# Two products of 256 columns become one of 512 in the edge sums, and VectorE adds the two halves of the bank

## The chip, the cores and the metric

The kernel runs on one NeuronCore of a Trainium2 chip. The time is the device time of one execution in microseconds, the median of three runs. The engines are TensorE (PE in the profile, its weight loads PEld), VectorE (DVE), ScalarE (ACT), GpSimd (POOL) and SyncE (SP, which only issues transfers here).

## The reference

Two graph layers, each followed by a feed-forward block, on 6250 nodes of 256 features and 100,000 edges:

```python
x = x + L0_gnn(layernorm(x), src, dst, edge_weight)   # segment_sum(w * (x @ Wl)[src]) + x @ Wr + biases
x = x + L0_ffn(layernorm(x))                          # 8 experts, softmax gates, two hidden layers, BN + relu
x = x + L1_gnn(layernorm(x), src, dst, edge_weight)   # segment_sum(w * (x @ W)[src]) + bias
x = x + L1_ffn(layernorm(x))                          # 32 experts, argmax picks one, relu
```

In both graph layers `out[n]` is the sum over the edges that end in node n of the edge's weight times the row of the edge's source node (`jax.ops.segment_sum`). All of it is float32.

## The kernel before

The edges are sorted so that the edges of 128 nodes stand together, padded to 784 tiles of 128 edges. A slot s takes U = 4 tiles, so there are EGROUPS = 196 slots. The code writes the order of every engine by hand, slot by slot: a Python loop over s emits for PE, VectorE and ScalarE what belongs to the slot, and semaphores tie the engines together. Nothing is scheduled afterwards.

An edge sum is a matrix product: for 128 edges, a one-hot matrix (edge by node) is the weight operand and the 128 gathered rows are the moving operand; the product adds 256 columns for 128 nodes into a PSUM bank. For precision each float32 operand is split into an upper part (rounded to fp32r) and a lower part (the rest), and the parts are multiplied apart.

**Second stage, names f_...** GpSimd gathers four times 128 rows a slot (L1408, an indirect DMA each, ring of four slots in `got`). ScalarE multiplies them by the edge weights (L1467) and writes the upper part `mhi` (L1476); VectorE writes the lower part `mlo` (L1683) and the one-hot `hot` (L1677). PE multiplies the same one-hot by `mhi` and then by `mlo` into `bank[6 + t % 2]`, columns 0 to 255 (L1584, L1585). Edges of one slot can belong to two node tiles, so some slots have 4 such pairs and some 8: 1168 in all. When tile t is complete, in slot 4t+5, VectorE adds the bank to the node's row (L1807) and runs the layer norm's statistics (L1809 to L1813). The first FFN runs beside the edges, one expert in two slots: PE L1397 to L1399 (layers of up to 512 columns and outputs of 256), ScalarE relu and upper part (L1492, L1497), VectorE lower part (L1689) and the gated output add (L1706). VectorE's lower messages free the ring slot for GpSimd. After the last edges the FFN goes on alone until about 1790 us.

**Last stage, names n_...** The gathered rows are already two-part: a table row is 512 wide, upper part then lower part. VectorE writes weighted one-hots, upper `hot_h` and lower `hot_l` (L2360, eight instructions of 128 columns a slot). For every edge tile PE runs three products of 256 columns: `hot_h` by the upper half, `hot_h` by the lower half, `hot_l` by the upper half (L2231 to L2233), so 784 of each. The sums run over windows of two slots and 128 nodes that overlap by half, in `bank[6 + m % 2]`. When window m closes, ScalarE copies one half of 64 partitions to `agg` (L2171, `s_half`) and VectorE adds the other half, whose copy came from the window before (L2378, `s_sum`). PE opens a bank again two windows later, behind `s_half` and `s_sum`. Beside it the second FFN runs from slot 13 on: PE hidden products (L2249 to L2253), ScalarE relu (L2184), VectorE lower part n_hrl (L2394), PE outputs (L2273 to L2277). GpSimd's gathers (L2120, ring of four slots) wait for PE's count of slots, `s_prod`.

Of the kernel before, what the change touches and what calls it, by code (L numbers as in the profile page):

```python
# [9 lines left out]
F32R = mybir.dt.float32r  # L10
# [3 lines left out]
ALU = mybir.AluOpType  # L14
# [18 lines left out]
U = 4  # L33
# [57 lines left out]
def build(nc, x, src, dst, wgt, wl, wr, bl, br, gw, gbr, w1, b1, g1, be1, m1, v1,  # L91
          w2, b2, g2, be2, m2, v2, wo, bo, lw, lb, rw, rb, mw1, mb1r, mw2, mb2, out):
    ctx = ExitStack()
    with ctx:
# [1115 lines left out]
        with ExitStack() as c3, nc.Block() as block:  # L1210
# [8 lines left out]
            s_accin = sem("f_accin")  # L1219
            s_sum = sem("f_sum")  # L1220
# [53 lines left out]
            mhi = sb3("mhi", [P, 2, U, D], F32R)  # L1274
            mlo = sb3("mlo", [P, 2, U, D], F32R)
# [86 lines left out]
            def tile_bank(t):  # L1362
                return bank[6 + t % 2][:, 0:D]
# [207 lines left out]
            def _(pe):  # L1571
                def edges(s):
# [6 lines left out]
                    for u in range(U):  # L1579
                        for t, at in node_tiles(s):  # L1580
# [3 lines left out]
                            nc.tensor.matmul(tile_bank(t), lhs, mhi[:, s % 2, u, :], start=begins, stop=False)  # L1584
                            last = nc.tensor.matmul(tile_bank(t), lhs, mlo[:, s % 2, u, :], start=False, stop=ends)  # L1585
# [82 lines left out]
            def _(dve):  # L1668
# [109 lines left out]
                for s in range(SLOTS):  # L1778
# [22 lines left out]
                    for g in range(NG):  # L1801
                        for k in range(width(g)):
                            t = tile(g, k)
                            if edges_end(t) == s:
                                dve.wait_ge(s_prod, s)
                                dve.wait_ge(s_accin, g * 16 + 16)
                                nc.vector.tensor_tensor(row(g, k), tile_bank(t), row(g, k), ALU.add).then_inc(s_sum, 1)  # L1807
# [93 lines left out]
        with ExitStack() as c4, nc.Block() as block:  # L1901
# [16 lines left out]
            s_half = sem("n1_half")  # L1918
            s_lw = sem("n1_lw")
# [149 lines left out]
            def window_bank(m):  # L2069
                return bank[6 + m % 2][:, 0:D]  # L2070
# [89 lines left out]
            def _(act):  # L2160
# [3 lines left out]
                for s in range(SLOTS):  # L2164
                    if s % 2 == 1 and s < EGROUPS:
# [5 lines left out]
                        nc.scalar.activation(agg[a:b, t % 2, :], window_bank(m)[a:b, :], ACT.Copy).then_inc(s_half, 1)  # L2171
# [46 lines left out]
            def _(pe):  # L2218
                def edges(s):
                    m = window_of(s)  # L2220
                    opens, closes = s == 0 or s % 2 == 1, s % 2 == 0 or s == EGROUPS - 1
                    if opens and m >= 2:
                        pe.wait_ge(s_half, m - 1)
# [4 lines left out]
                    for u in range(U):  # L2228
                        w_h, w_l = hot_h[:, s % HOTS, u, :], hot_l[:, s % HOTS, u, :]
                        m_h, m_l = (got[:, s % RING, u, a:a + D] for a in (0, D))  # L2230
                        nc.tensor.matmul(window_bank(m), w_h, m_h, start=(opens and u == 0), stop=False)  # L2231
                        nc.tensor.matmul(window_bank(m), w_h, m_l, start=False, stop=False)  # L2232
                        last = nc.tensor.matmul(window_bank(m), w_l, m_h, start=False, stop=(closes and u == U - 1))  # L2233
# [105 lines left out]
            def _(dve):  # L2339
# [32 lines left out]
                for s in range(SLOTS):  # L2372
                    m = (s - 1) // 2
                    if s % 2 == 1 and 1 <= m < WINDOWS:
                        t, (a, b) = halves(m)[1]
                        dve.wait_ge(s_prod, min(s, EGROUPS))
                        dve.wait_ge(s_half, m)
                        nc.vector.tensor_tensor(agg[a:b, t % 2, :], window_bank(m)[a:b, :], agg[a:b, t % 2, :],  # L2378
                                                ALU.add).then_inc(s_sum, 1)
# [144 lines left out]
```

## Time and profile before

| | |
|---|---|
| median of 3 runs | 3136.0 us (3130.68 to 3143.77) |
| the profiled execution, its own time | 3133.19 us |
| span of its instructions | 3131.3 us |
| PE busy | 2684.4 us, 86% |
| PEld (weight loads) | 2474.8 us, 79% |
| DVE busy | 2161.1 us, 69% |
| ACT busy | 1557.7 us, 50% |
| POOL busy | 1971.0 us, 63% |
| mean granted TensorE clock | 0.929 |

Busy time is the union of an engine's instructions; the reported ends of matmuls are modelled and overlap the next one, so the distance between starts tells what a product costs. "Idle before" names what the engine waited for; "issue" is a wait for which the profile shows nothing, "remote" one for a releaser that it could not name.

### The profile page before, as it was taken

The page shows a single profiled execution, that of the slowest core. Times are in us where ns is not written, and L with a number is a line of the kernel's source. Part 1 is how long each engine was busy: PE and PEld are TensorE (multiplying, and loading weights), DVE is VectorE, ACT ScalarE, POOL GpSimd, SP SyncE. Part 2 cuts the span into 40 slices and gives each one's busy share as a digit, 9 for nine tenths or more (in the row PEclk, how much of TensorE's full clock was granted, in tenths as well). Part 3 has the DMA queues.
Part 4 walks back from the last instruction along what each step waited for, and adds up shares of the span by engine and source line. Part 5 has one row for each costly group of instructions (what it writes and reads, how often), then busy time and mean ns, then how long its engine had stood idle before and what let it go on. Part 6 is the DMA issues. An engine that isn't in the chain of part 4 may idle for free. (4 is left out here: it accounts for less than half of the span.)

```text
span 3131.3 us, 54480 instructions
## 1 busy us (share of the span) xinstructions
PE 2684.4 (86%) x19092; PEld 2474.8 (79%) x19092; DVE 2161.1 (69%) x5110; ACT 1557.7 (50%) x3295; POOL 1971.0 (63%) x1696
## 2 busy tenths in 40 slices
PE   5899826899999999999999737888888989888889
PEld 5788725798888888888888626788888888888889
DVE  8888654588787878778876565665666666666663
ACT  3477555788888888888886410111111111111112
POOL 0455467678888888888880076666666666666660
PEclk9999957899999999999999967899998999899999
DMA  2143453233333332333231176767776776767760
GB/s 70 6 94 77 101 156 105 82 93 110 93 101 109 108 111 83 110 108 112 86 110 35 36 226 172 183 172 179 179 178 172 179 175 176 181 176 179 178 171 13
DMA packets 241962, 390.31 MB, mean 125 GB/s; under 512 B 43642, under 2 KB 115218, under 8 KB 241426
## 3 DMA queue, kind: packets, MB, share of 16 engines
q0 software_dynamic: 163072, 310.24, 38.6%
q1 hardware_dynamic: 78324, 74.90, 7.7%
q8 instruction: 156, 2.56, 0.3%
q10 hardware_dynamic: 288, 1.61, 0.1%
q14 instruction: 122, 1.00, 0.1%
HBM read 343.43 MB, written 43.19 MB: 123 GB/s over the span
## 5 line engine op out<-in xcount | busy, mean ns | idle before, releaser
L1408 POOL DMA_INDIRECT f_got<-h_tab,list_cols x784 | 991.5, 1265 | 251.4 <-issue 221.3
L2120 POOL DMA_INDIRECT n_got<-h_tab,edge_cols x784 | 807.9, 1031 | 427.9 <-issue 220.5
L2184 ACT ACTIVATE n_hrh<-bank 128x512 fp32r<-128x512 f32 x196 | 117.0, 597 | 644.3 <-DMA list<-runs,off_i 355.0
L1689 DVE TENSOR_TENSOR f_hlo<-edge_cols,f_hhi 128x1024 fp32r<-128x1024 f32 (+1 forms) x208 | 241.9, 1163 | 259.6 <-ACT f_hhi L1497 189.1
L2394 DVE SCALAR_TENSOR_TENSOR n_hrl<-bank,n_hrh 128x512 fp32r<-128x512 f32 x196 | 135.1, 689 | 379.6 <-ACT n_hrh L2184 305.8
L1467 ACT ACTIVATE f_got<-f_got,list_cols 128x256 f32<-128x256 f32 x784 | 333.4, 496 | 116.3 <-DMA f_got<-h_tab,list_cols 110.9
L1584 PE MATMUL bank<-f_mhi,f_hot 128*128 128x256 f32 x1168 | 307.3, 296 | 56.9 <-DVE f_mlo L1683 50.6
L1492 ACT ACTIVATE edge_cols<-bank,f_shf,f_scl 128x512 f32<-128x512 f32 (+1 forms) x416 | 292.1, 743 | 94.4 <-PE bank L1399 39.7
L2231 PE MATMUL bank<-n_got,n_hot_h 128*128 128x256 f32 x784 | 244.0, 311 | 79.9 <-DMA n_got<-h_tab,edge_cols 36.7
L1585 PE MATMUL bank<-f_mlo,f_hot 128*128 128x256 f32 x1168 | 305.4, 295 | 3.5 <-issue 3.5
L400 POOL DMA_INDIRECT list<-runs,off_i x98 | 159.9, 1631 | 217.5 <-DVE off_i L759 100.4
L1584 PEld LDWEIGHTS bank<-f_mhi,f_hot 128*128 128x128 f32 x1168 | 235.3, 201 | 63.5 <-issue 59.5
L2249 PE MATMUL bank<-n_xnh,n_w1h 128*128 128x256 f32 (+1 forms) x800 | 238.4, 298 | 22.0 <-ACT n_ohT L2206 11.8
L1397 PE MATMUL bank<-f_whi,f_hhi 128*128 128x256 f32 x784 | 230.2, 294 | 27.5 <-DVE f_hlo L1689 19.2
L1683 DVE TENSOR_TENSOR f_mlo<-f_got,f_mhi 128x1024 fp32r<-128x1024 f32 x196 | 238.7, 1218 | 17.7 <-ACT f_mhi L1476 17.3
L2275 PE MATMUL bank<-n_w2l,n_hrh 128*128 128x256 f32 x784 | 229.3, 292 | 24.4 <-issue 24.3
L2251 PE MATMUL bank<-n_xnh,n_w1l 128*128 128x256 f32 (+1 forms) x800 | 236.2, 295 | 11.1 <-issue 10.8
L2273 PE MATMUL bank<-n_w2h,n_hrh 128*128 128x256 f32 x784 | 230.0, 293 | 17.8 <-issue 17.3
L2250 PE MATMUL bank<-n_xnl,n_w1h 128*128 128x256 f32 (+1 forms) x800 | 236.5, 296 | 6.6 <-issue 6.4
L1585 PEld LDWEIGHTS bank<-f_mlo,f_hot 128*128 128x128 f32 x1168 | 235.1, 201 | 8.7 <-issue 5.0
L2360 DVE TENSOR_SCALAR n_hot_h<-list_cols,rel_f,edge_cols 128x128 fp32r<-128x128 f32 x784 | 220.4, 357 | 28.3 <-remote 17.8
L2277 PE MATMUL bank<-n_w2h,n_hrl 128*128 128x256 f32 x784 | 227.6, 290 | 13.7 <-issue 12.9
(329 smaller groups left out, 7882.4 us busy)
## 6 DMA issues: line engine op xcount, KB each, us to landing
f_got<-h_tab,list_cols POOLq DMA_INDIRECT x784
n_got<-h_tab,edge_cols POOLq DMA_INDIRECT x784
n_rows<-acc_tab SPq DMA_DIRECT2D x24, 256.0 KB
out_rows<-n_rows SPq DMA_DIRECT2D x24, 256.0 KB
h_tab<-acc SPq DMA_DIRECT2D x37, 128.0 KB
edge_cols<-in_w SPq DMA_DIRECT2D x16, 256.0 KB
acc<-in_x SPq DMA_DIRECT2D x4, 896.0 KB
h_tab<-hbuf SPq DMA_DIRECT2D x7, 512.0 KB
```

Source lines behind the costliest of these rows:

```text
L1408: nc.gpsimd.indirect_dma_start(got[:, s % RING0, u, :], None, h_tab[0], bass.IndirectOffsetOnAxis(gidx0[:, s * U + u:s * U + u + 1], 0), b ...
L1467: last = nc.scalar.activation(got[:, s % RING0, u, :], got[:, s % RING0, u, :], ACT.Copy, scale=w0_f[:, c:c + 1])
L1492: nc.scalar.activation(rl[:, m, 0:w], bank[(i + m) % 3][:, 0:w], ACT.Relu, bias=shf[:, l, e, m:m + 1], scale=scl[:, l, e, m:m + 1]).then_i ...
L1584: nc.tensor.matmul(tile_bank(t), lhs, mhi[:, s % 2, u, :], start=begins, stop=False)
L1585: last = nc.tensor.matmul(tile_bank(t), lhs, mlo[:, s % 2, u, :], start=False, stop=ends)
L1683: nc.vector.tensor_tensor(mlo[:, s % 2, :, :], got[:, s % RING0, :, :], mhi[:, s % 2, :, :].bitcast(F32), ALU.subtract).then_inc(s_mlo, 1)
L1689: nc.vector.tensor_tensor(hlo[l][:, :, 0:w], rl[:, :, 0:w], hhi[l][:, :, 0:w].bitcast(F32), ALU.subtract).then_inc(s_lo[l], 1)
L2120: nc.gpsimd.indirect_dma_start(got[:, s % RING, u, :], None, h_tab[1], bass.IndirectOffsetOnAxis(gidx[:, s * U + u:s * U + u + 1], 0), bou ...
L2231: nc.tensor.matmul(window_bank(m), w_h, m_h, start=(opens and u == 0), stop=False)
L2249: nc.tensor.matmul(to, hi_w, hi_x, start=(f == 0), stop=False)
L2250: nc.tensor.matmul(to, hi_w, lo_x, start=False, stop=False)
L2251: nc.tensor.matmul(to, lo_w, hi_x, start=False, stop=False)
```

## The change

In the second stage upper and lower messages lie side by side in one tile `msg`, and one product of 512 columns writes a whole bank: columns 0 to 255 get the upper part's sum, 256 to 511 the lower part's. VectorE adds first the one half of the bank to the row, then the other, with a wait between them (`s_upsum`). In the last stage `hot_h` meets the whole gathered row in one product of 512 columns, and `hot_l` the upper half as before into columns 0 to 255. ScalarE copies its half of the partitions from columns 0 to 255. VectorE then adds, for each window: columns 0 to 255 of the half it has always added; columns 256 to 511 of the half that ScalarE copied (`s_low`, behind `s_half` of the same window); columns 256 to 511 of its own half (`s_sum`). PE opens the bank again behind `s_low` and `s_sum`.

```diff
-            mhi = sb3("mhi", [P, 2, U, D], F32R)
-            mlo = sb3("mlo", [P, 2, U, D], F32R)
+            msg = sb3("msg", [P, 2, U, 2 * D], F32R)
+            mhi, mlo = (msg[:, :, :, i * D:(i + 1) * D] for i in range(2))
...
-                            nc.tensor.matmul(tile_bank(t), lhs, mhi[:, s % 2, u, :], start=begins, stop=False)
-                            last = nc.tensor.matmul(tile_bank(t), lhs, mlo[:, s % 2, u, :], start=False, stop=ends)
+                            last = nc.tensor.matmul(tile_bank(t)[:, :], lhs, msg[:, s % 2, u, :], start=begins, stop=ends)
...
-                                nc.vector.tensor_tensor(row(g, k), tile_bank(t), row(g, k), ALU.add).then_inc(s_sum, 1)
+                                nc.vector.tensor_tensor(row(g, k), tile_bank(t)[:, 0:D], row(g, k), ALU.add).then_inc(s_upsum, 1)
+                                dve.wait_ge(s_upsum, t + 1)
+                                nc.vector.tensor_tensor(row(g, k), tile_bank(t)[:, D:2 * D], row(g, k), ALU.add).then_inc(s_sum, 1)
...
-                        nc.scalar.activation(agg[a:b, t % 2, :], window_bank(m)[a:b, :], ACT.Copy).then_inc(s_half, 1)
+                        nc.scalar.activation(agg[a:b, t % 2, :], window_bank(m)[a:b, 0:D], ACT.Copy).then_inc(s_half, 1)
...
-                        pe.wait_ge(s_half, m - 1)
+                        pe.wait_ge(s_low, m - 1)
...
-                        m_h, m_l = (got[:, s % RING, u, a:a + D] for a in (0, D))
-                        nc.tensor.matmul(window_bank(m), w_h, m_h, start=(opens and u == 0), stop=False)
-                        nc.tensor.matmul(window_bank(m), w_h, m_l, start=False, stop=False)
-                        last = nc.tensor.matmul(window_bank(m), w_l, m_h, start=False, stop=(closes and u == U - 1))
+                        ends = closes and u == U - 1
+                        nc.tensor.matmul(window_bank(m)[:, :], w_h, got[:, s % RING, u, :], start=(opens and u == 0),
+                                         stop=ends, skip_group_check=True)
+                        last = nc.tensor.matmul(window_bank(m)[:, 0:D], w_l, got[:, s % RING, u, 0:D], start=False,
+                                                stop=ends, skip_group_check=True)
...
-                    if s % 2 == 1 and 1 <= m < WINDOWS:
-                        t, (a, b) = halves(m)[1]
+                    if s % 2 == 1 and m < WINDOWS:
+                        copied, added = halves(m)
                         dve.wait_ge(s_prod, min(s, EGROUPS))
-                        dve.wait_ge(s_half, m)
-                        nc.vector.tensor_tensor(agg[a:b, t % 2, :], window_bank(m)[a:b, :], agg[a:b, t % 2, :],
-                                                ALU.add).then_inc(s_sum, 1)
+                        if added:
+                            t, (a, b) = added
+                            rest = agg[a:b, t % 2, :]
+                            dve.wait_ge(s_low, m)
+                            nc.vector.tensor_tensor(rest, window_bank(m)[a:b, 0:D], rest, ALU.add).then_inc(s_upsum, 1)
+                        if copied:
+                            t, (a, b) = copied
+                            dve.wait_ge(s_half, m + 1)
+                            nc.vector.tensor_tensor(agg[a:b, t % 2, :], window_bank(m)[a:b, D:2 * D], agg[a:b, t % 2, :],
+                                                    ALU.add).then_inc(s_low, 1)
+                        if added:
+                            t, (a, b) = added
+                            dve.wait_ge(s_upsum, m)
+                            nc.vector.tensor_tensor(rest, window_bank(m)[a:b, D:2 * D], rest, ALU.add).then_inc(s_sum, 1)
```

PE, last stage, the edges of one slot in the midst of the run (n_hot_h and n_hot_l are the one-hots, n_got the gathered rows). Before, the first two of its four edge tiles:

```order
L2231 MATMUL bank<-n_got,n_hot_h 128x256
L2232 MATMUL bank<-n_got,n_hot_h 128x256
L2233 MATMUL bank<-n_got,n_hot_l 128x256
L2231 MATMUL bank<-n_got,n_hot_h 128x256
L2232 MATMUL bank<-n_got,n_hot_h 128x256
L2233 MATMUL bank<-n_got,n_hot_l 128x256
```

Now the last three of the four, and the first output product of the FFN behind them:

```order
L2235 MATMUL bank<-n_got,n_hot_h 128x512
L2237 MATMUL bank<-n_got,n_hot_l 128x256
L2235 MATMUL bank<-n_got,n_hot_h 128x512
L2237 MATMUL bank<-n_got,n_hot_l 128x256
L2235 MATMUL bank<-n_got,n_hot_h 128x512
L2237 MATMUL bank<-n_got,n_hot_l 128x256
L2278 MATMUL bank<-n_w2h,n_hrh 128x256
```

A slot's twelve edge products have become eight; nothing around them moved.

VectorE, last stage, the start of an odd slot, in which a window closes (n_agg is the sum of a tile, n_xnl belongs to the slot before). Before:

```order
L2431 TENSOR_TENSOR n_xnl<-list_cols,n_xnh 128x2x128
L2378 TENSOR_TENSOR n_agg<-bank,n_agg 64x256
L2360 TENSOR_SCALAR n_hot_h<-list_cols,rel_f,edge_cols 128x128 x4
L2360 TENSOR_SCALAR n_hot_l<-list_cols,rel_f,edge_cols 128x128 x4
L2394 SCALAR_TENSOR_TENSOR n_hrl<-bank,n_hrh 128x512
```

Now:

```order
L2447 TENSOR_TENSOR n_xnl<-list_cols,n_xnh 128x2x128
L2386 TENSOR_TENSOR n_agg<-bank,n_agg 64x256
L2390 TENSOR_TENSOR n_agg<-bank,n_agg 64x256
L2395 TENSOR_TENSOR n_agg<-bank,n_agg 64x256
L2365 TENSOR_SCALAR n_hot_h<-list_cols,rel_f,edge_cols 128x128 x4
L2365 TENSOR_SCALAR n_hot_l<-list_cols,rel_f,edge_cols 128x128 x4
L2410 SCALAR_TENSOR_TENSOR n_hrl<-bank,n_hrh 128x512
```

Two more adds stand ahead of the one-hots and of n_hrl.

VectorE, second stage, a slot in which a tile is complete (f_msg holds both parts of the messages, f_xlo belongs to the FFN's next group). Before:

```order
L1677 TENSOR_TENSOR f_hot<-xn,rel_f 128x4x128
L1683 TENSOR_TENSOR f_mlo<-f_got,f_mhi 128x1024
L1799 TENSOR_TENSOR f_xlo<-edge_cols,f_xhi 128x1024
L1807 TENSOR_TENSOR acc<-bank,acc 128x256
L1809 BN_STATS f_stats<-acc 128x6
```

Now, in the same slot:

```order
L1677 TENSOR_TENSOR f_hot<-xn,rel_f 128x4x128
L1683 TENSOR_TENSOR f_msg<-f_got,f_msg 128x4x256
L1799 TENSOR_TENSOR f_xlo<-edge_cols,f_xhi 128x1024
L1807 TENSOR_TENSOR acc<-bank,acc 128x256
L1809 TENSOR_TENSOR acc<-bank,acc 128x256
L1811 BN_STATS f_stats<-acc 128x6
```

The second add stands between the first and the statistics; the lower messages (L1683) now go out in four pieces of 256.

## Rows read from the trace of the kernel before

**Rows 1.** The page, busy time of each engine.
```profile
PE 2684.4 (86%) x19092; PEld 2474.8 (79%) x19092; DVE 2161.1 (69%) x5110; ACT 1557.7 (50%) x3295; POOL 1971.0 (63%) x1696
```

**Rows 2.** Stretches: length, busy PE, PEld, DVE, ACT, POOL, clock, DMA share, GB/s.
```profile
1100.00:1600.00 500.00, 474.42 (x2977) 422.75 (x2977) 405.31 (x686) 437.25 (x701) 403.41 (x317) 0.99 0.35 105
2000.00:2500.00 500.00, 446.43 (x3300) 424.17 (x3299) 313.72 (x1110) 82.03 (x216) 321.26 (x316) 0.94 0.70 177
2500.00:3000.00 500.00, 441.82 (x3273) 422.25 (x3272) 311.57 (x1105) 82.55 (x217) 322.08 (x317) 0.94 0.71 178
3050.00:3131.00 81.00, 77.87 (x646) 76.78 (x645) 29.29 (x83) 16.29 (x37) 1.09 (x2) 1.00 0.07 20
```

**Rows 3.** Line L1408, 1100 to 1600 us: ns, idle before it, who waited.
```profile
L1408 POOL DMA_INDIRECT f_got<-h_tab,list_cols x317: 1011/1017/2821, 1099.6 to 1598.7; - x159
...
  issue: 89.9, 295
  DVE f_mlo L1683: 6.7, 22
...
  ACT f_got L1467: 29.6, 27
```

**Rows 4.** Timeline, 461 and 1151 us: start, length, engine, line.
```profile
461.70 0.42 DVE L1807 TENSOR_TENSOR acc<-bank,acc 128x256 f32<-128x256 f32 x1
461.84 1.01 POOL L1408 DMA_INDIRECT f_got<-h_tab,list_cols  x1 [0.30 <-DVE f_mlo L1683]
...
1151.53 1.22 DVE L1683 TENSOR_TENSOR f_mlo<-f_got,f_mhi 128x1024 fp32r<-128x1024 f32 x1
...
1152.20 1.43 POOL L1408 DMA_INDIRECT f_got<-h_tab,list_cols  x1 [0.30 <-issue]
...
1152.66 0.42 DVE L1807 TENSOR_TENSOR part<-bank,part 128x256 f32<-128x256 f32 x1
...
1153.12 0.43 DVE L1809 BATCH_NORM_STATS2 f_stats<-part 128x6 f32<-128x256 f32 x1
```

**Rows 5.** Waits of POOL and DVE, 2000 to 2500 us: us, times, longest.
```profile
DVE n_hrl L2394 <- ACT n_hrh L2184: 112.3, 36, 6.6
...
POOL n_got L2120 <- remote: 57.4, 27, 2.5
...
POOL n_got L2120 <- PE bank L2233: 32.8, 21, 2.8
```

**Rows 6.** Waits of PE, 2000 to 2500 us.
```profile
PE bank L2275 <- issue: 10.4, 16, 1.0
...
PE bank L2249 <- ACT n_ohT L2206: 6.7, 3, 3.2
```

**Rows 7.** Timeline, 2070 to 2075 us.
```profile
2070.41 0.38 ACT L2171 ACTIVATE n_agg<-bank 64x256 f32<-64x256 f32 x1 [1.46 <-remote]
2070.42 0.42 DVE L2378 TENSOR_TENSOR n_agg<-bank,n_agg 64x256 f32<-64x256 f32 x1 [0.96 <-remote]
...
2073.95 0.28 PE L2232 MATMUL bank<-n_got,n_hot_h 128*128 128x256 f32 x1 [0.33 <-issue]
...
2074.65 0.28 PE L2233 MATMUL bank<-n_got,n_hot_l 128*128 128x256 f32 x1 [0.41 <-issue]
```

**Rows 8.** Groups of instructions, whole span: count, busy us, mean ns, idle before.
```profile
L1585 PE MATMUL bank<-f_mlo,f_hot 128*128 128x256 f32 x1168 | 305.4, 295 | 3.5 <-issue 3.5
...
L2232 PE MATMUL bank<-n_got,n_hot_h 128*128 128x256 f32 x784 | 230.0, 293 | 7.0 <-issue 6.9
...
L2378 DVE TENSOR_TENSOR n_agg<-bank,n_agg 64x256 f32<-64x256 f32 x98 | 41.2, 420 | 39.4 <-remote 31.9 <-PE bank L2233 5.7
```

**Rows 9.** Timeline of PE, first and last of each run of even steps.
```profile
1199.77 0.39 PE L1398 MATMUL bank<-f_hlo,f_whi 128*128 128x512 f32 x1
...
1202.06 0.40 PE L1399 MATMUL bank<-f_hhi,f_wlo 128*128 128x512 f32 x1
...
1210.53 0.28 PE L1584 MATMUL bank<-f_mhi,f_hot 128*128 128x256 f32 x1
...
1211.48 0.28 PE L1397 MATMUL bank<-f_whi,f_hhi 128*128 128x256 f32 x1
```

More of the change, by code:

```diff
@@ L1219, in build @@
             s_accin = sem("f_accin")
+            s_upsum = sem("f_upsum")
             s_sum = sem("f_sum")
@@ L1362, in tile_bank @@
             def tile_bank(t):
-                return bank[6 + t % 2][:, 0:D]
+                return bank[6 + t % 2]
             def out_tile(k):
@@ L1918, in build @@
             s_half = sem("n1_half")
+            s_upsum = sem("n1_upsum")
+            s_low = sem("n1_low")
             s_lw = sem("n1_lw")
@@ L2069, in window_bank @@
             def window_bank(m):
-                return bank[6 + m % 2][:, 0:D]
+                return bank[6 + m % 2]
             def halves(m):
```

## The prediction

> **What bounds the kernel now.** I read the page first: TensorE (PE) is busy 86% of the span, VectorE (DVE) 69%, ScalarE (ACT) 50%, GpSimd (POOL) 63% [rows 1]. The average hides two different regimes, so next come the stretches. The change touches the "f" stage (edge sums of the first layer with the first FFN beside them, edges from about 410 to 1660 us) and the "n" stage (second layer, about 1812 to 3131 us).
>
> In the f stage, 1100 to 1600 us, PE is busy 474 of 500 us at clock 0.99, DVE 405, ACT 437, POOL 403 [rows 2]. POOL looks idle for a fifth of the time, but it is not: its waits are 89.9 us "issue" (295 times 0.30 us, the step between two gathers) and only 6.7 us for DVE [rows 3]. 403.4 + 89.9 = 493.3 of 500 us, so the issue of gathers sets the pace: 317 gathers, four to a slot, 6.31 us a slot. Behind it ACT waited for gathered rows 27 times, 29.6 us [rows 3]. PE's idle time is 25.6 us; it waits for ACT and DVE results of the FFN, which come late behind the gathers. Why a gather costs POOL 1.27 us there: its median is 1.017 us and its longest 2.82 [rows 3]. Where VectorE runs f_mlo (both operands in SBUF) while a gather starts, the gather ends 0.9 us after f_mlo does (1153.63 against 1152.75) and takes 1.43 us; where VectorE runs the add that reads a bank, it takes 1.01 us [rows 4]. So VectorE's operations on two SBUF operands stretch the gathers, and those with a bank operand don't.
>
> In the n stage, 2000 to 2500 us, 316 gathers make 79 slots of 6.33 us. PE is busy 446 us, its clock 0.94; DVE 314, ACT 82, POOL 321 [rows 2]. POOL waits there for PE: 57.4 (its "remote" is PE's count as well, the only thing it can wait for) + 32.8 us [rows 5], so PE leads. But 53.6 us of PE's idle time is mostly "issue" (the longest line 10.4 us), waits for which the profile shows no releaser; a real one is 6.7 us for ACT [rows 6]. They come in clusters while gathers run without a pause: two successive products start at 2073.95 and 2074.65, 0.70 us apart in place of 0.12, with nothing awaited [rows 7]. After the gathers end the stage has none of this: from 3050 us PE is busy 77.9 of 81 us at clock 1.00 [rows 2].
>
> **The change part by part.** PE. Each pair of 256-column products on the same weights becomes one of 512: 1168 pairs in f, 784 in n (196 slots of 4), and as many weight loads go [rows 8]. The reported 0.28 and 0.39 us of a product overlap its neighbours, so the price is the distance between starts. 256 columns: eight steps from 1210.53 to 1211.48, 0.119 us. 512 columns, same weight shape: ten steps from 1199.77 to 1202.06, 0.229 us [rows 9]. A pair costs 0.238 and the one product 0.229: 0.009 saved. The columns streamed are the same; only what a second start costs is saved. With the rounding of the starts (0.01 us over 8 and 10 steps) it lies between 0.007 and 0.011; I take 0.010.
> In f that is 1168 x 0.010 = 11.7 us of PE time. Until 1653 us it lies beside POOL, which is full. It counts 0, with a bound of 11.7 if PE turned out to set the pace. The FFN steps after the last edges have no such pair.
> In n it is 784 x 0.010 = 7.8 us. The second FFN does not begin before slot 13; until then PE has 12 short products a slot (1.4 us) against four gathers (5.2 us), so 13 x 4 pairs are hidden: 7.3 us on the path.
>
> The unexplained waits of n. A slot has 3300/79 = 41.8 products; the change takes 4 of them, 9.6%. Idle 53.6 and 58.2 us in the two stretches of 500 us [rows 2], less 6.7 us for ACT in the first and about as much in the second, is 98 us in 1000; the clock of 0.94 (12% of the time at half rate) adds 30 us in 500. Over the 1050 us from 2000 to 3050 that makes about 166 us. If these waits belong to PE's instruction count, 9.6% of it goes: 16 us. If they belong to the stream of gathers, which stays as it is, nothing goes. The trace does not decide. That the waits are gone where the gathers are [rows 2], and that the bytes moved are alike in both stretches (177 and 178 GB/s), speaks for the gathers. I take a third, 5 us, and keep 0 and 16 as ends.
>
> VectorE, f stage. One more add of the form bank + SBUF row, 128x256, for each of 49 tiles: 0.42 us, and 0.46 from its start to that of the next, dependent one (1152.66 to 1153.12 [rows 4]): 49 x 0.46 = 22 us. It stands behind f_mlo of the slot and ahead of bn_stats, where only the tile's own chain waits. Its operand is a bank, so by rows 4 it leaves the gathers alone. DVE has 95 of 500 us idle. Cost 0; if the cover were gone, up to 22 us. f_mhi and f_mlo are now written in pieces of 256 elements that lie 512 apart, the number of elements being the same; I count nothing for it. A tenth on f_mlo's 1.22 us would stretch 196 gathers by 0.12 us, 24 us: that is its upper end.
>
> VectorE, n stage. Before, one add of 64 partitions for a window, now three: 98 + 98 + 98, so 196 more at 0.42 (0.46 with the step), 90 us [rows 8]. It takes DVE from 314 to about 350 of 500 us. The order within an odd slot: add, add (behind ACT's copy of the same window), add, then the one-hots two slots ahead, then n_hrl. Queued behind the new wait are the one-hots and n_hrl. Two adds make n_hrl 0.9 us later; by the code PE asks for the n_hrl of slot s in slot s + 1, behind that slot's edges. DVE's largest idle time is before just this n_hrl, 112.3 us for ACT [rows 5], and it swallows the adds. ACT's copy (0.38 us) starts with DVE's first add, 2070.41 and 2070.42 [rows 7], so the new wait on it is empty. PE used to wait for the copy and the add, and now for one add more, two slots ahead of need: no cost. For the first windows, where slots are short, I count 1 us.
>
> Sum: 0 - 7.3 - 5 + 0 + 1 = -11.3 us. The profiled run took 3133.2 us (span 3131.3), which gives 3121.9. The median before is 3136.0, 2.8 us above the profiled run, so I forecast 3125 us.
>
> **The rivals.** (A) PE gains count in full: the waits without releaser shrink with the instruction count (16 us), and in f PE's 11.7 us is worth something because POOL, ACT and PE are within 5% of each other. For: PE is busy 95% in f. Against: POOL's 493.3 of 500. It gives -7.8 - 16 to -7.8 - 16 - 11.7, so 3100 to 3112 us.
> (B) Slower: the 0.455 us added in the 49 sum slots of f pushes the next two-SBUF operations (f_hot, f_mlo) onto the start of a gather that they now miss. The price is that of rows 4: 0.42 us for a gather that started 0.67 us into f_mlo, and up to 1.09 for one that starts with it. If each sum slot had one more blocked start, 49 x 0.42 to 1.09 = 21 to 53 us, less 12: 3145 to 3177 us. It decides from about two blocked starts in three sum slots on. Against: gathers are already stretched by 0.25 us on average, four to a slot, and a shift makes as many starts free as it blocks.
>
> (C) The n stage is paced by the gathers and not by PE: its 177 and 178 GB/s are what it gets. Then a faster PE only waits more, and the change gives 0 to -3 us: 3133 to 3136. For: the even rate. Against: POOL stands waiting for PE 90 of 500 us.
> The Trainium skill, "Runtime: NRT & Kernel Launch", section on instruction fetch mechanics, says that blocks of 256 instructions are fetched ahead and that crossing one is mostly hidden; by that the waits would not come from PE's instruction stream and the 5 us would be 0 (3130). No row here names their cause.
>
> **How the numbers follow.** My forecast 0.40, (A) 0.27, (B) 0.13, (C) 0.20. The measurement tells 0.5% (15.7 us) from no change, so faster begins below 3120.3 us and slower above 3151.7. Faster: most of (A), 0.25, and a quarter of the forecast's own spread (3112 to 3131), 0.10. Slower: two thirds of (B), and a little for a VectorE chain that is tighter than I see, 0.12. The rest, 0.53, is no change. The range: the forecast, (C), (A) down to 3102 and the lower part of (B), 3102 to 3148.
>
> **What would show it.** Right: starts of the 512-column products 0.227 to 0.230 us apart and 0.35 us for 512 plus 256 in n; gathers of f still at a mean near 1.27 us and POOL's issue plus busy near 493 of 500; PE's idle share in f higher by about 1 point; the f stage as long as before within 5 us; DVE up by some 36 us in 2000 to 2500 with no PE wait for n_agg; slots of n near 6.27 us. Wrong: PE waits "for DVE n_agg"; f_msg lines that hold the gathers longer (mean above 1.30); an n slot below 6.2 us, which would be (A); PE's waits for gathered rows in n, which would be (C); or steps of 0.238 us and more for the 512 columns.

## The result, and the profile after

| | before | after |
|---|---|---|
| median, on the same chip | 3143.4 us (7 runs, 3130.7 to 3155.2) | 3123.7 us (7 runs, 3115.7 to 3132.2) |
| ratio to before | 1 | 0.9946 (0.9923 to 0.9970) |
| the profiled execution | 3133.2 us | 3132.2 us |

The change makes the kernel 0.54% faster, 17 us by the ratio and 20 us by the medians. The forecast was 3125 us, 11 us less than before. The two profiled executions differ by 1 us only: that of after was the slowest of its seven runs. Their gathers, first start to last, take 1241.4 us before and 1238.1 after in f (the second stage), 1237.1 and 1236.5 in n (the last stage). So the two profiles tell what an operation costs and who waits for whom, and the 17 us have to be found with more runs.

The page of the kernel after, busy time of each engine (to [rows 1]):

```profile
PE 2679.6 (86%) x17140; PEld 2368.7 (76%) x17140; DVE 2264.5 (72%) x5355; ACT 1561.0 (50%) x3295; POOL 1966.8 (63%) x1696
```

PE has 1952 products fewer, 1168 + 784, and 4.8 us less busy time; DVE has 103 us more. The stretches of [rows 2], after:

```profile
1100.00:1600.00 500.00, 468.32 (x2481) 393.17 (x2480) 407.04 (x695) 432.85 (x693) 401.10 (x312) 0.98 0.34 104
2000.00:2500.00 500.00, 442.64 (x2961) 413.40 (x2960) 345.23 (x1173) 82.56 (x214) 317.88 (x315) 0.91 0.70 176
2500.00:3000.00 500.00, 447.90 (x2996) 413.27 (x2995) 350.16 (x1200) 84.04 (x220) 324.00 (x318) 0.92 0.70 178
```

In f, PE is idle 6 us more in 500 (474.4 became 468.3 busy). POOL issues 312 gathers in this stretch where it issued 317, but over the whole stage it is 3 us quicker, so no change of its pace can be read from that. In n, DVE has 31.5 us more in 500 and the same number of gathers goes through; PE's clock is 0.91 where it was 0.94. The f gathers of after in 1100 to 1600 us (to [rows 3]: least, median and longest ns, then the waits before them, then who waited for them):

```profile
L1409 POOL DMA_INDIRECT f_got<-h_tab,list_cols x312: 1007/1016/3232, 1099.4 to 1598.9; - x156
...
  issue: 89.7, 289
  DVE f_msg L1683: 9.5, 23
...
  ACT f_got L1468: 30.2, 29
```

401.1 + 89.7 = 490.8 of 500 us (493.3 before): POOL is still full, and its wait grew by 3 us. What a product of 512 columns costs, on PE's timeline of after in n (start, reported length, line):

```profile
2084.24 0.40 PE L2235 MATMUL bank<-n_got,n_hot_h 128*128 128x512 f32 x1
2084.47 0.28 PE L2237 MATMUL bank<-n_got,n_hot_l 128*128 128x256 f32 x1
2084.59 0.39 PE L2235 MATMUL bank<-n_got,n_hot_h 128*128 128x512 f32 x1
2084.82 0.27 PE L2237 MATMUL bank<-n_got,n_hot_l 128*128 128x256 f32 x1
2084.93 0.40 PE L2235 MATMUL bank<-n_got,n_hot_h 128*128 128x512 f32 x1
```

From 2084.24 to 2084.93 are two tiles, 0.345 us each, of which about 0.232 us for the 512 columns. Over all tiles of the stage the median step from L2235 to L2237 is 0.235 us, in f from one L1585 to the next 0.233; the median step of 256 columns before is 0.120. A pair saves 0.005 to 0.007 us, some 0.006, and not the 0.010 that I took: 5 us in n.

One wait is new, at the start of each group of the second FFN. Waits of PE after, 2000 to 2500 us (to [rows 6]):

```profile
PE bank L2254 <- ACT n_ohT L2210: 30.0, 8, 4.5
PE bank L2280 <- issue: 9.2, 12, 1.0
PE bank L2282 <- issue: 6.4, 11, 1.0
PE bank L2278 <- issue: 4.5, 6, 0.9
```

n_ohT is the one-hot of the chosen experts, ScalarE's last copy before a group's hidden products. PE waited 6.7 us for it in [rows 6] and 30.0 us here, 47.1 us over the stage against 11.8. (The expectations below speak of 98 us against 26: these add the waits of PE's weight loads, 51.2 and 14.6 us, which are largely the same time.) PE's waits without releaser fell at the same time, from 45.8 to 26.7 us in 2000 to 2500. Which of the two is the change's doing is a question for the runs.

POOL and VectorE after (to [rows 5]):

```profile
POOL n_got L2124 <- remote: 52.9, 24, 2.5
POOL n_got L2124 <- PE bank L2237: 46.3, 35, 2.3
```
```profile
DVE n_hrl L2410 <- ACT n_hrh L2188: 119.4, 50, 5.4
```

VectorE still stands 119 us for ScalarE before n_hrl, with 31.5 us more work. What became shorter are its other waits: those for a releaser without a name before n_agg (17.6 to 3.0 us) and before n_rows (13.1 us to none), and those without releaser before n_hrl (22.1 to 11.9). So the added adds seem to lie in idle time, though not in the wait for ScalarE.

### The profile page after: what moved, and what is told of

Its sections match the earlier page's. It is cut to its first block and busy times, and to the rows that moved or that the text cites. A ratio compares the mean times of both kernels' runs of the same rounds, so it can differ in the third digit from the quotient of the medians.

```text
span 3130.2 us, 50822 instructions
## 1 busy us (share of the span) xinstructions
PE 2679.6 (86%) x17140; PEld 2368.7 (76%) x17140; DVE 2264.5 (72%) x5355; ACT 1561.0 (50%) x3295; POOL 1966.8 (63%) x1696
## 5 line engine op out<-in xcount | busy, mean ns | idle before, releaser
L2235 PE MATMUL bank<-n_got,n_hot_h 128*128 128x512 f32 x784 | 326.8, 445 | 79.7 <-DMA n_got<-h_tab,edge_cols 35.5
L1585 PE MATMUL bank<-f_msg,f_hot 128*128 128x512 f32 x1168 | 325.3, 416 | 56.4 <-DVE f_msg L1683 48.1
L1585 PEld LDWEIGHTS bank<-f_msg,f_hot 128*128 128x128 f32 x1168 | 226.3, 201 | 107.8 <-issue 62.1
L2254 PE MATMUL bank<-n_xnh,n_w1h 128*128 128x256 f32 (+1 forms) x800 | 241.4, 302 | 58.2 <-ACT n_ohT L2210 47.1
L1683 DVE TENSOR_TENSOR f_msg<-f_got,f_msg 128x1024 fp32r<-128x1024 f32 x196 | 238.5, 1217 | 19.3 <-ACT f_msg L1477 17.8
L2235 PEld LDWEIGHTS bank<-n_got,n_hot_h 128*128 128x128 f32 x784 | 163.4, 208 | 115.6 <-issue 52.2
L2237 PE MATMUL bank<-n_got,n_hot_l 128*128 128x256 f32 x784 | 232.7, 297 | 2.2 <-issue 2.2
L2365 DVE TENSOR_SCALAR n_hot_l<-list_cols,rel_f,edge_cols 128x128 fp32r<-128x128 f32 x784 | 226.5, 369 | 0.0
```

What stands on the lines that cost most here:

```text
L1585: last = nc.tensor.matmul(tile_bank(t)[:, :], lhs, msg[:, s % 2, u, :], start=begins, stop=ends)
L2235: nc.tensor.matmul(window_bank(m)[:, :], w_h, got[:, s % RING, u, :], start=(opens and u == 0), stop=ends, skip_group_check=True)
L2237: last = nc.tensor.matmul(window_bank(m)[:, 0:D], w_l, got[:, s % RING, u, 0:D], start=False, stop=ends, skip_group_check=True)
L2254: nc.tensor.matmul(to, hi_w, hi_x, start=(f == 0), stop=False)
```

## The experiments

The first eight kernels ran on one chip (A) and the last four on another (B). Both are slower than the first: before takes 3189 to 3191 us on A and 3178 us on B. Only runs of one chip, or ratios to before on the same chip, are compared. The theories: **T**, mine: f is paced by POOL and gives nothing, all comes from n, the adds are hidden. **Rivals**: both stages give something (A of the prediction); n is paced by the gathers (C); the adds delay ScalarE and so cause the wait for n_ohT.

### Each stage alone

`e1_f_only` has the change in f and the code of before in n. `e2_n_only` is the other way round. Their diffs are the two parts of the diff above.

> Only the f stage is changed, the n stage is that of before. My theory (the issue of gathers sets the pace of f, 493 of 500 us, so PE's shorter pairs are hidden): 0 against before, at most 3 us either way; f gathers end within 4 us of before's (1242.5 us from first to last), gather mean near 1.26 us. Rival (A), PE's gain counts in f: -8 to -12 us, and the gathers end that much earlier. Rival (B), the added add stretches gathers: +20 us or more and a gather mean above 1.30.

> Only the n stage is changed. My theory: all of the difference of the changed kernel is here, so -11 to -20 us against before, as the whole change. Rival: the gain is split between the stages, then about half, -8 to -10 us. If the new waits of PE for ACT's n_ohT (98 us in the profile of the changed kernel against 26 us for the same step before) were a cost of their own, this kernel would be no faster than before.

Measured, with the whole change on the same chip: f alone 0.9963 (0.9933 to 0.9994, 12 runs), n alone 0.9943 (0.9918 to 0.9969, 12 runs), both 0.9922 (0.9893 to 0.9951, 8 runs):

> The changed kernel again, on the same chip as the experiments. From the two halves alone (0.9963 with f changed, 0.9943 with n changed) the sum is 0.9906; the first comparison gave 0.9946. If the stages add up, 0.989 to 0.993 here. My theory of step f = 0 gives 0.9943 (the n part alone).

So f gives some 12 us (between 2 and 21), n some 18 us (10 to 26), and the sum of the two, 0.9906, fits the 0.9922 of both. T is probably wrong on f, but not surely: the 2 us are within its "at most 3", and the interval of both holds its 0.9943 as well. The first and last gather of each stage (min/median/max ns, first and last start), f only, then n only, then both:

```profile
L1409 POOL DMA_INDIRECT f_got<-h_tab,list_cols x784: 1007/1015/3297, 408.0 to 1668.4; - x196
L2122 POOL DMA_INDIRECT n_got<-h_tab,edge_cols x784: 998/1004/3016, 1832.2 to 3094.6; - x196
```
```profile
L1408 POOL DMA_INDIRECT f_got<-h_tab,list_cols x784: 1006/1014/2859, 412.2 to 1685.8; - x196
L2122 POOL DMA_INDIRECT n_got<-h_tab,edge_cols x784: 997/1003/3532, 1852.4 to 3093.0; - x196
```
```profile
L1409 POOL DMA_INDIRECT f_got<-h_tab,list_cols x784: 1006/1014/2825, 410.4 to 1680.8; - x196
L2124 POOL DMA_INDIRECT n_got<-h_tab,edge_cols x784: 997/1003/3532, 1851.0 to 3094.2; - x196
```

n's gathers take 1262.4 us with the old products, 1240.6 and 1243.2 with the new ones: 20 us. (The two profiles of the first chip show 1 us of this.) f's take 1260.4 and 1270.4 with the new code, 1273.6 with the old: here two profiles of the same code differ by 10 us. The eight profiles of chip A have new code in f five times (mean 1265.8 us, 1258.5 to 1271.7) and old three times (1275.5, 1272.2 to 1280.7).

Where f loses time on this chip: POOL's waits from 500 to 1600 us, n only (f as before), then f only:

```profile
POOL f_got L1408 <- issue: 197.7, 622, 2.0
POOL f_got L1408 <- DVE f_mlo L1683: 69.1, 52, 8.7
```
```profile
POOL f_got L1409 <- issue: 197.7, 627, 2.0
POOL f_got L1409 <- DVE f_msg L1683: 51.4, 53, 8.2
```

The kernels before and after on the first chip have 26.8 and 22.3 us in that row. In this window POOL stands 2 us or longer, up to 9, in 14, 16 and 18 places in three profiles with f as before, and in 9, 10 and 13 places in three with f changed (1 and 2 on the first chip). The profile of both changes on chip A has 69.4 us in the row, as much as n only, so the row alone does not prove the gain. What such a place looks like: at 618 us in the profile of n only, gathers go on while PE starts its products 0.7 and then 1.4 us apart with nothing awaited, and ScalarE and VectorE stand as well:

```profile
618.29 0.39 PE L1398 MATMUL bank<-f_hlo,f_whi 128*128 128x512 f32 x1
...
619.01 0.48 PE L1399 MATMUL bank<-f_hhi,f_wlo 128*128 128x512 f32 x1 [0.33 <-issue]
...
620.43 0.48 PE L1397 MATMUL bank<-f_hhi,f_whi 128*128 128x512 f32 x1 [0.94 <-issue]
...
621.87 0.59 PE L1398 MATMUL bank<-f_hlo,f_whi 128*128 128x512 f32 x1 [0.96 <-issue]
...
630.53 1.06 ACT L1476 ACTIVATE f_mhi<-f_got 128x1024 fp32r<-128x1024 f32 x1 [10.70 <-remote]
```

This is what [rows 7] show in n. I read it so: after such a stop PE is late, POOL's ring is full, and then a lighter PE stream counts. That is argued from these places and not shown apart. My sum looked at a stretch with 6.7 us of such waits [rows 3] and priced f at 0 from it.

### The n stage without the added adds

```diff
-                            nc.vector.tensor_tensor(rest, window_bank(m)[a:b, 0:D], rest, ALU.add).then_inc(s_upsum, 1)
-                            nc.vector.tensor_tensor(agg[a:b, t % 2, :], window_bank(m)[a:b, D:2 * D], agg[a:b, t % 2, :],
-                                                    ALU.add).then_inc(s_low, 1)
-                            nc.vector.tensor_tensor(rest, window_bank(m)[a:b, D:2 * D], rest, ALU.add).then_inc(s_sum, 1)
+                            dve.sem_inc(s_low, 1)
+                            nc.vector.tensor_tensor(rest, window_bank(m)[a:b, 0:D], rest, ALU.add).then_inc(s_sum, 1)
```

> The n stage changed as above, but VectorE's three sums a window are one again: columns 256 to 511 of the bank are added nowhere (the output lacks the lower halves), PE's products are those of the changed kernel. My theory (the added adds lie in VectorE's idle time ahead of n_hrl): the same as with the n stage changed, within 3 us. Rival (the adds make VectorE and, behind it, ACT late, and PE's waits for n_ohT come from that): 10 to 25 us faster than with the n stage changed, and PE's waits for n_ohT fall from some 98 us back to some 26.

Measured: 0.9947 (0.9919 to 0.9975), against 0.9943 with the adds; n gathers in 1243.7 us against 1240.6. In 1900 to 3000 us, with the adds and without:

```profile
1900.00:3000.00 1100.00, 952.77 (x6218) 868.19 (x6218) 749.54 (x2563) 176.01 (x459) 706.72 (x695) 0.91 0.71 176
```
```profile
1900.00:3000.00 1100.00, 952.88 (x6222) 868.43 (x6223) 677.03 (x2386) 174.23 (x458) 704.50 (x692) 0.91 0.70 175
```

72.5 us less of VectorE changes nothing: the same 952.8 us of PE, the same clock. The adds are hidden, within some 9 us, and the rival's 10 to 25 us did not come. PE's waits for n_ohT over the stage are 18.1 us with the adds and 9.3 without. That is within what profiles of one and the same code differ by (4.0 to 47.1 us, below), so the adds are not shown to cause these waits, nor cleared of a part in them.

### How much PE's time is worth in each stage

`e4_f_half` is before without the product with the lower messages in f:

```diff
-                            nc.tensor.matmul(tile_bank(t), lhs, mhi[:, s % 2, u, :], start=begins, stop=False)
-                            last = nc.tensor.matmul(tile_bank(t), lhs, mlo[:, s % 2, u, :], start=False, stop=ends)
+                            last = nc.tensor.matmul(tile_bank(t), lhs, mhi[:, s % 2, u, :], start=begins, stop=ends)
```

> The kernel before without the product with the lower messages in the f stage (1568 - 400 = 1168 products of 256 columns fewer, one of each pair; the lower parts are summed nowhere). PE has 1168 x 0.119 = 139 us less in f. My theory (POOL's issue of gathers paces f where nothing disturbs it): f's gathers end only by the 30 to 55 us earlier that POOL stood waiting for f_mlo beyond a step (on this chip), so 30 to 60 us faster. Rival (PE paces f): 100 us and more faster.

Measured: 0.9934 (0.9895 to 0.9973), 21 us for 139 us of PE. f's gathers take 1246.8 us (chip B; 1265.0 with the code of before). The 21 us (9 to 33) are less than the 30 to 60 that I expected and far from the 100 of the rival. PE's pace does not set f's: T holds in this.

`e5_n_two` is before with two products a tile in n:

```diff
-                        nc.tensor.matmul(window_bank(m), w_h, m_l, start=False, stop=False)
-                        last = nc.tensor.matmul(window_bank(m), w_l, m_h, start=False, stop=(closes and u == U - 1))
+                        last = nc.tensor.matmul(window_bank(m), w_h, m_l, start=False, stop=(closes and u == U - 1))
```

> The kernel before with two products for each gathered tile of the n stage in place of three (hot_h with the upper half is left out): 784 products of 256 columns fewer, 93 us of PE at 0.119 us, and 10% of its instructions. Theory 1 (PE leads in n, its stalls don't depend on its count): 85 to 95 us faster, stalls of over twice a step as before, some 250 us. Theory 2 (stalls shrink with the instruction count): 110 to 125 us faster. Rival (C), gathers pace n: within 20 us of before.

(The expectation names the wrong product: `hot_l` by the upper half is left out. Number and length are as it says.)

Measured: 0.9938 (0.9916 to 0.9961), 20 us for 93 us of PE: just what rival (C) allowed, and far below both theories. I had PE leading in n, because POOL waits for it 90 us in 500 [rows 5]; it does not. With 93 us less of PE, POOL waits for it almost as long:

```profile
POOL n_got L2120 <- remote: 65.3, 29, 2.7
POOL n_got L2120 <- PE bank L2232: 13.0, 11, 2.5
```

Two stretches of n, e5:

```profile
2000.00:2500.00 500.00, 435.85 (x2973) 408.78 (x2972) 312.00 (x1111) 81.05 (x214) 325.56 (x318) 0.88 0.71 177
2500.00:3000.00 500.00, 428.42 (x2995) 405.79 (x2996) 310.97 (x1104) 84.25 (x220) 321.85 (x317) 0.90 0.72 178
```

Four products a slot less, and the slot is as long as in [rows 2], on the first chip (318 gathers for 316); PE's clock is 0.88. To see where the 93 us went I sorted PE's time from the first to the last edge product of n by the distance between two starts: up to a step at full clock ("work"), the rest of a distance of up to twice that step ("slow steps", mostly the half clock), and the rest of longer ones ("stops"):

| us | chip | work | slow steps | stops | sum |
|---|---|---|---|---|---|
| n as before (f only) | A | 896 | 104 | 265 | 1265 |
| n changed (n only) | A | 891 | 94 | 257 | 1243 |
| n changed (both) | A | 891 | 88 | 267 | 1246 |
| n as before (e4) | B | 896 | 95 | 266 | 1257 |
| n changed (both) | B | 891 | 93 | 263 | 1247 |
| two products (e5) | B | 803 | 113 | 318 | 1234 |

Of 93 us of work taken out, 52 came back as stops and 18 as slow steps (with a slightly different step taken as full clock, 44 and 24). The change takes out 5 us of work and gives 10 to 22. The change and e5 take out the same 784 products with their weight loads, the one almost without their time, the other with it, and the whole kernels gain the same, 0.9943 (n only, chip A) and 0.9938 (chip B), each within some 8 us. In f it is alike: 0.9963 for 1168 products without their time, 0.9934 with it, the intervals overlapping. So the time that the products take is worth little, and what the change gives is more likely tied to their number. No kernel takes out products alone or weight loads alone, so which of the two it would be is not shown. That is the 16-us end of my "unexplained waits", though not as I argued it: the stops do not shrink with the count (265 to 257 and 267 us). On chip A the slow steps shrink by 10 and 16 us, on B by 2.

With the instructions go their fetches. The trace lists them as a DMA queue of its own; queue q8 over the whole run (packets, MB, share), before and after:

```profile
q8 instruction: 156, 2.56, 0.3%
```
```profile
q8 instruction: 140, 2.29, 0.3%
```

Its packets have 16 KB each, and their number follows PE's instructions: 16 fewer for 1952 products and as many weight loads, 6 fewer in e5 for 784 and 784. The stops do not lie on these fetches. In the kernel before PE stands in stops 16% of the time from 2000 to 3040 us, but 7% of the time of the 55 such packets (after 15% and 6%, e6 below 18% and 8%), counted from the packets' times. An effect some time before or behind a fetch is not excluded by that.

### What the stops of n hang on

Three kernels try the stream of gathers. In `e6_n_narrow` (before) a gather brings 256 columns a row and not 512, of other rows, and all three products use them:

```diff
-                            got[:, s % RING, u, :], None, h_tab[1],
+                            got[:, s % RING, u, 0:D], None, h_tab[1].rearrange("n (a d) -> (n a) d", d=D),
...
-                        m_h, m_l = (got[:, s % RING, u, a:a + D] for a in (0, D))
+                        m_h, m_l = (got[:, s % RING, u, a:a + D] for a in (0, 0))
```

> The kernel before, whose n gathers bring 256 columns a row in place of 512 (half the bytes; another half row stands where the lower message stood, so the values are others). Instructions of all engines are the same. Theory 1 (the stalls come from a DMA queue that is never empty): a gather of half the bytes lands 1.4 us after its issue, as in f, the queue falls empty nearly each time, PE's stalls go from some 250 us to under 80 us, and the n stage becomes gather-issue bound, 196 x 5.24 us = 1030 us against 1240: up to 200 us faster. Theory 2 (stalls belong to PE's instruction count): within 20 us of before.

Measured: 0.9989 (0.9962 to 1.0017), nothing. From 2000 to 2500 us:

```profile
2000.00:2500.00 500.00, 438.84 (x3183) 415.83 (x3182) 303.40 (x1077) 79.33 (x209) 316.94 (x311) 0.92 0.41 92
```

DMA share 0.41 for 0.70, 92 GB/s for 177, and the slot and the stops (265 us) are as they were. The queue was emptied as meant: a packet of the gathers is under way 54% of the time from 2000 to 3000 us and was 88%. So neither the bytes nor a queue that is never empty makes the stops, and my theory 1 is out. The number of row packets is the same (some 90,000 in that time), so a cause in their number is not tested.

Where the stops lie is told by the packed traces. From 2000 to 3040 us, with a pause of GpSimd of over 0.45 us ending a row of gathers, PE stands in stops 0 to 7% of the time in the first 8 us of a row and 58% from 8 to 10 us; in e6 it is 1 to 12% and 61%. A row also ends because PE has stopped and the ring is full, so this tells when the stops come and not that the row causes them.

In `e8_pause` and `e9_landed` (after) POOL waits, before a slot's gathers, until three or all four gathers of the slot before have landed. In e8 the fourth gather has a semaphore of its own, `s_fourth`, on which PE waits as well; e9 waits for `16 * U` of `s_got`.

```diff
+                    if s:
+                        pool.wait_ge(s_got[(s - 1) % RING], ((s - 1) // RING + 1) * (16 * (U - 1)))
```

> The changed kernel, but in the n stage GpSimd starts a slot's four gathers only when the first three of the slot before have landed (about 0.7 us of pause every four gathers, by the 2.3 us from issue to landing). What it tells: in the profiles PE stands in stalls 1 to 5% of the time in the first 7 us of a row of gathers without a pause and 50 to 75% of it after 8 us. Theory 1 (PE's unexplained waits come from gathers that follow each other without a pause of the DMA queue): shorter bursts take most of the 240 us of stalls away and the slot goes from 6.3 to about 6.0 us, 30 to 60 us faster than the changed kernel. Theory 2 (they belong to PE's own instructions or a period of its own): stalls as before, time the same or up to 20 us slower.

> As above, but GpSimd waits until all four gathers of the slot before have landed, a pause of some 2.0 us every four gathers. Both theories: a slot becomes 4 x 1.31 + 2.0 = 7.2 us and more, so 170 to 200 us slower. Theory 1: PE's stalls of over twice its step vanish but for waits on the gathered rows. Theory 2: the waits without a releaser stay at 40 us or so in 500.

Measured: 1.0483 (1.0449 to 1.0517) and 1.1303 (1.1252 to 1.1354), some 176 and 438 us slower than the changed kernel on this chip and far outside of every expectation. Waits of POOL and then all waits of PE from 2000 to 2500 us, first e8, then e9:

```profile
POOL n_got L2128 <- DMA n_got<-h_tab,edge_cols: 155.5, 69, 3.1
...
PE bank L2240 <- DMA n_got<-h_tab,edge_cols: 71.4, 34, 4.2
PE bank L2240 <- issue: 34.8, 20, 5.1
```
```profile
POOL n_got L2126 <- DMA n_got<-h_tab,edge_cols: 210.2, 59, 4.4
...
PE bank L2237 <- DMA n_got<-h_tab,edge_cols: 155.5, 58, 5.5
```

POOL stands 3.56 us a time in e9 (210.2 / 59) and 2.25 us in e8 (155.5 / 69), which is 1.31 us less, one gather's step. In e9, over 195 slots, the last packet of the fourth gather ends 2.5 us after the gather's instruction on POOL has ended, and the next gather starts another 1.1 us later: so much a wait on a landing cost beyond the last byte, and the expectations had left it out. The slots become 8.6 us in e9 and 7.3 in e8, and PE waits for rows. The scattered "issue" waits are gone from PE in e9, as theory 1 said, and stand on one line in e8. Both the pauses and the slack that they give PE could have done that, so the two kernels don't tell which.

### The second FFN one slot later

```diff
-            AT_AGG, AT_PROD, AT_SUM, AT_NORM, AT_TURN, AT_LOG, AT_PICK, AT_MASK, AT_FFN = range(1, 10)
+            AT_AGG, AT_PROD, AT_SUM, AT_NORM, AT_TURN, AT_LOG, AT_PICK, AT_MASK, AT_FFN = (*range(1, 9), 10)
```

> The changed kernel with the second FFN's groups started one slot later behind their tiles (ready slot + 10 in place of + 9), so that ACT's copy n_ohT has 6.3 us more before PE asks for it. Theory 1 (the waits for n_ohT only take the place of waits that PE would have had anyway while ACT and PE stand still in the gather bursts): PE's n_ohT wait goes to under 10 us, its unexplained waits rise by as much, time within 5 us of the changed kernel, or 3 to 6 us slower since the last FFN group starts a slot later. Theory 2 (the 98 us are a cost of their own): 20 to 60 us faster than the changed kernel.

Measured on chip A: 0.9876 (0.9839 to 0.9914), with both at 0.9922. Since that was not side by side, both ran again on chip B:

> The changed kernel once more beside the next one: 0.992 of before, as in the run before this.

> The changed kernel with the second FFN's groups a slot later, again, now on the same chip at the same time as the changed kernel. If the waits for n_ohT are a cost of their own, it is 10 us and more faster than the changed kernel; if they take the place of other stalls, within 6 us.

Measured: the changed kernel 0.9935 (0.9911 to 0.9958, median 3161.3 us), one slot later 0.9918 (0.9893 to 0.9943, 3150.3 us). The side-by-side runs differ by 9.5 us in the mean, 8 us either way; over both chips, 14 runs against 12, it is 12.9 us, some 6 either way. So this version beats both kernels, by some 0.3 to 0.4% against the changed one. It lies between what the two theories had said (within 5 or 6 us; 20 to 60, then 10 and more). PE's waits for n_ohT, changed kernel on A, then on B (the whole n stage):

```profile
PE bank L2254 <- ACT n_ohT L2210: 4.0, 7, 1.5
```
```profile
PE bank L2254 <- ACT n_ohT L2210: 15.4, 8, 4.3
```

The same code had 47.1 us in the first profile, so this wait comes and goes between executions; one slot later L2254 has no such row. But the wait is not what was gained: on chip A it was 4.0 us and the later kernel is 15 us faster there. Which slack the later start gives, and to whom, is open. The n gathers of the later kernel take 1236.0 and 1232.6 us against 1243.2 and 1244.2, 7 to 12 us less. The profiles also have f shorter by 12 to 16 us, where the code is the same; I take that for the scatter of f, since nothing in f was edited.

## Why the prediction was right, and where it was not

The time was right (3125 forecast, 3123.7 found); the ratio says 17 us, the sum said 11. That the two times meet within 2 us is luck. The forecast started from 3136.0, the median of three runs; the seven runs beside the changed kernel gave 3143.4, and from there the sum comes to 3132. Inside the sum, a term for PE's time that was too high stood against a term for the waits that was too low. By its steps:

- **A pair in one product, 0.010 us.** Too much: some 0.006, just outside my bracket of 0.007 to 0.011.
- **f costs and gives 0.** Probably wrong by about 10 us (2 to 21 on chip A; the first chip's profiles have 3 us). POOL is full (490.8 of 500), and 139 us less of PE gave only 21, so PE's time is worth as little as I said. What f gave comes, as far as the places where POOL stands tell, from stops of the stage that my stretch of 500 us hardly had.
- **n, 7.3 us of PE's time on the path.** The mechanism failed: PE does not lead there. 93 us taken out gave 20, so by that rate the 5 us saved are worth about 1 (an estimate). On the first chip a slot of n took 6.31 us in both profiles, where I had forecast 6.27.
- **The unexplained waits, 5 us out of 0 to 16.** Mis-sized: n alone gave 18 us (10 to 26), of which at most 5 are PE's time. The upper end was right as a number; which waits went is not the same on the two chips.
- **VectorE's adds, 0.** Right: 72.5 us less changed nothing. DVE rose by 31.5 of the 36 forecast. Its wait for ScalarE before n_hrl, which I had swallow the adds, stayed (112.3 and 119.4 us); other waits of VectorE became shorter.
- **f_msg in pieces, 0.** Right: the operation takes 1.217 us against 1.218, the mean gather of f 1.263 us against 1.265. The reading of [rows 4] holds for the stage: 107 gathers that start under f_mlo take 1.96 us in the median and end 0.89 us after it, 113 that start under an operation with a bank operand take 1.01 us; after the change it is 1.96 and 0.89 again.
- **Nothing new waits, 1 us for the first windows.** The wait on ScalarE's copy is empty (n_agg's L2390 is idle 3.0 us in 98 before it starts, the step between two dependent adds). PE waits once for the new add, 3.7 us at the start of the stage, where it had waited once for ScalarE's copy, 3.8 us. I did not foresee n_ohT.

Of the rivals, (A) was nearest in kind: both stages give. But its price for f, 11.7 us of PE time in full, is the wrong reason for about the right number. (B) did not come: the mean gather did not grow. (C) was half right: n does not follow PE; but it does not follow the bytes either. The Trainium skill ("Runtime: NRT & Kernel Launch", instruction fetch mechanics) says that crossing from one fetched block to the next is mostly hidden. The equal gains for equal counts speak against it, and the stops that neither shrink with the count nor lie on the fetches speak for it; no run here decides.

Open: what makes PE, ScalarE and VectorE stop for some microseconds while gathers are issued. The stops are gone where the gathers are (on the first chip PE has none from 3060 us on). They need neither the gathers' bytes nor the added work of VectorE, and they grow when PE has less to do (266 to 318 us). The number of row packets and the fetches are rivals that no kernel varied alone. Open too is why n gives 18 us where 5 us of work go.

## What to carry to other kernels

- An engine for which another one waits is not yet the one that leads. The test is to take a tenth of its work out and look at the time: here 93 us of PE gave 20 in n, where the rest came back as stops and slow steps, and 139 gave 21 in f.
- Fusing two products on the same weights gave little in engine time (0.006 us a pair) and still gave 18 us in n, as much as taking the products out with their time. The adds that it puts on another engine cost nothing measurable here, since VectorE had 186 of 500 us idle.
- Where an engine asks for a result just as it comes, try a slot of slack. It is an edit of one line, and here it gave 0.3 to 0.4%, though not by the wait for which it was meant.

## What the runs showed that was not expected

- Halving the bytes of 784 gathers (177 to 92 GB/s) changed the time by less than 0.4% either way.
- A wait of GpSimd on landed gathers cost 1.1 us beyond the last byte (e9), which comes 2.5 us after the gather's instruction has ended.
- The same kernel took 3143, 3190 and 3178 us on three chips, and the f stage of the same code differed by 10 us and more between profiled executions. Edits worth less than that are told apart by medians of many runs, not by two profiles.
